# The first stretch of a decoder layer: a small table spread by the scalar engine, and the first batch's rotations on the vector engine

## The reference, cut to what matters

```python
def attn(x, Wq, Wkv_down, Wk_up, Wv_up):          # 16 heads of 32
    q = (x @ Wq)...                                # heads of 32: 8 plain numbers, 24 rotated ones
    c_kv = x @ Wkv_down                            # width 128
    k, v = (c_kv @ Wk_up)..., (c_kv @ Wv_up)...
    q_rope, k_rope = rope(q_rope), rope(k_rope)    # xe*cos - xo*sin, xo*cos + xe*sin
    scores = q @ k.T * scale, causal
    return softmax(scores) @ v
x = layernorm(x + attn(x))
x = layernorm(x + xattn(x, ctx))                   # top 54 of 512 keys
x = layernorm(x + ffn(x))                          # 8 experts, the first NL = 2 with low-rank additions
# gate[:NL] += x @ Ga @ Gb, up[:NL] += x @ Ua @ Ub, out[:NL] += mid @ Da @ Db
```

## Time and profile before

| | us |
|---|---|
| median of 3 runs | 1692.59 (1692.43 to 1700.83) |
| profiled execution | 1692.4 |
| its span | 1690.6 |
| start stretch, up to the first DVE instruction of the loop | 0 to 109.25 |

### The profile page before, as it was taken

How to read it: one execution, slowest core, us unless ns; L and a number is a source line. 1 busy time by engine, 2 the same in 40 slices (tenths; PEclk the granted TensorE clock), 3 DMA queues, 4 the chain that set the end, 5 groups by cost and what they waited for, 6 DMA issues and landing times.

```text
span 1690.6 us, 26867 instructions
## 1 busy us (share of the span) xinstructions
PE 1443.2 (85%) x9924; PEld 869.5 (51%) x9924; DVE 1273.0 (75%) x2115; ACT 903.6 (53%) x1431; POOL 846.8 (50%) x724
## 2 busy tenths in 40 slices
PE   4767787776668988848799999999999999999984
PEld 2345545444544444423356655666566655665553
DVE  4849899899867999975957767767766766766757
ACT  3327566565664544445455565556555565556542
POOL 6418385564352123687644654456454654466421
PEclk9969898989779999968999999999999999999997
DMA  9050010000211010110001000100101100100002
GB/s 282 26 200 2 28 51 2 28 26 27 100 51 50 26 70 32 51 63 13 25 26 38 26 26 29 35 26 26 37 26 31 33 26 26 38 26 26 13 1 100
DMA packets 63105, 74.62 MB, mean 44 GB/s; under 512 B 6912, under 2 KB 40320, under 8 KB 61952
## 3 DMA queue, kind: packets, MB, share of 16 engines
q1 hardware_dynamic: 62400, 68.68, 12.1%
q10 hardware_dynamic: 576, 4.19, 0.6%
HBM read 49.66 MB, written 10.49 MB: 36 GB/s over the span
## 4 chain that ended last, share of the span: by engine, by line
PE 60%; DVE 24%; issue 11%; ACT 3%; POOL 2%; DMA 1%; SPq 0%; DVEq 0%; POOLq 0%; ACTq 0%
PE banks L1103 48%; PE banks L870 6%; DVE nmf L1473 5%; DVE plo L1487 2%; PE banks L935 1%; DVE cat L1456 1%; PE banks L923 1%; DVE top L1599 1%; DVE wk L1595 1%; DVE att L1497 1%; DVE kcT L1463 1%; DMA w_fold<-w_top 1%; DVE attf L1606 1%; PE banks L1058 1%; DVE qcT L1483 1%
## 5 line engine op out<-in xcount | busy, mean ns | idle before, releaser
L1103 PE MATMUL banks<-xc,w 128*128 128x512 f16 x2688 | 591.2, 382 | 17.7 <-ACT banks L1144 15.0
L1103 PEld LDWEIGHTS banks<-xc,w 128*128 128x128 f16 x2688 | 264.2, 99 | 339.2 <-ACT banks L1144 20.2
L1103 PE MATMUL banks<-wd,mid 128*128 128x256 f16 x2688 | 298.1, 273 | 5.4 <-ACT banks L1144 3.1
L1103 PEld LDWEIGHTS banks<-wd,mid 128*128 128x128 f16 x2688 | 263.6, 98 | 40.9 <-ACT banks L1144 3.4
L847 POOL TENSOR_TENSOR mid<-m,mid 128x512 f16<-128x512 f32 x64 | 75.1, 1174 | 318.2 <-ACT mid L1144 318.2
L753 POOL TENSOR_TENSOR plo<-pf,phi 128x896 f16<-128x896 f32 x64 | 133.5, 2088 | 175.3 <-ACT phi L1144 175.2
L1144 ACT ACTIVATE banks<-banks 128x512 f32<-128x512 f32 x192 | 108.7, 579 | 193.0 <-PE banks L1103 193.0
L847 POOL TENSOR_TENSOR mid<-msum,mid 128x512 f16<-128x512 f32 x128 | 186.4, 1475 | 2.6 <-ACT mid L1144 2.6
L1421 DVE SCALAR_TENSOR_TENSOR w<-stage,w 128x512 f16<-128x512 f32 (+1 forms) x56 | 61.5, 1138 | 106.0 <-ACT w L1144 106.0
L1144 ACT ACTIVATE mid<-msum 128x512 f16<-128x512 f32 x128 | 81.2, 635 | 84.1 <-DVE msum L1780 28.1
L1473 DVE TENSOR_REDUCE nmf<-banks 128x1 f32<-128x512 f32 (+3 forms) x256 | 107.3, 480 | 14.9 <-PE banks L937 14.4
(11 more groups left out here) (252 smaller groups left out, 2910.8 us busy)
## 6 DMA issues: line engine op xcount, KB each, us to landing
stage<-w_fold SPq DMA_DIRECT2D x24, 256.0 KB, 3.0
stage<-in_Wg SPq DMA_DIRECT2D x24, 256.0 KB, 3.1
stage<-in_Wu SPq DMA_DIRECT2D x24, 256.0 KB, 3.1
stage<-in_Wd SPq DMA_DIRECT2D x24, 256.0 KB, 2.8
vcat<-vnext SPq DMA_DIRECT2D x8, 528.0 KB, 3.2
x_in<-in_x SPq DMA_DIRECT2D x4, 1024.0 KB, 6.3
x_res<-in_x SPq DMA_DIRECT2D x4, 1024.0 KB, 5.6
c_raw<-in_ctx SPq DMA_DIRECT2D x4, 1024.0 KB, 5.6
```

What stands on the lines that cost most here:

```text
L1103: mm = nc.tensor.matmul(out, l(x, i), r(y, i), start=start and i == 0 and j == 0, stop=stop and i == k - 1 and j == 2, skip_group_check=True)
```

## The change

Two edits.

1. POOL sets a table of only 4x16 (`own_small`), and ACT spreads it over the 512 columns of each head with one instruction of 4x8192. This stands in ACT's queue behind the four weights and ahead of `fold.0`. The sum of the semaphore `own_rows` is 3 instead of 2.
2. The eight rotations of the first batch are DVE's. POOL keeps those of the other three batches. `A_START_DVE` is written anew: eight `rope` steps are added, and `rlo`, `fold.0`, `v` and `cat0` stand in another order. The lists of PE and ACT for the stretch are the same.

```diff
 A_START_DVE = steps("""
-    half.0 half.1 c.0 rlo.0 rlo.1 fold.0 v.0 rlo.2 half.2 fold.1 v.1 rlo.3 half.3 fold.2 v.2 rlo.4 half.4 fold.3 rlo.5
-    half.5 fold.4 fold.5 cat0.0 cat0.1 cat0.2 cat0.3 cat0.4 rlo.6 cat0.5 rlo.7 cat0.6 cat0.7 maxn.0 maxn.1 maxn.2
-    maxn.3 v.3 mTn.0 maxn.4
+    half.0 half.1 rope.0 c.0 rope.1 rlo.0 fold.0 v.0 rope.2 rlo.1 half.2 rope.3 rlo.2 fold.1 v.1 rope.4 rlo.3 half.3 fold.2
+    v.2 rope.5 rlo.4 half.4 fold.3 rope.6 rlo.5 half.5 fold.4 rope.7 fold.5 cat0.0 rlo.6 cat0.1 cat0.2 cat0.3 rlo.7 cat0.4
+    cat0.5 cat0.6 cat0.7 maxn.0 maxn.1 maxn.2 maxn.3 v.3 mTn.0 maxn.4
 """)
...
-            own_row = kcT[K3:K3 + G, :, :].rearrange("p (g j) n -> p g j n", j=G)
+            own_row = own_small[K3:K3 + G, :].rearrange("p (g j) -> p g j", j=G)
             pool.wait_ge(consts, 14)
-            pool.memset(kcT[K3:K3 + G, :, :], 0.0).then_inc(own_rows, 1)
+            pool.memset(own_small[K3:K3 + G, :], 0.0).then_inc(own_rows, 1)
             pool.wait_ge(own_rows, 1)
             pool.affine_select(out=own_row, in_=own_row, compare_op=ALU.not_equal, fill=SNM, base=0,
-                               pattern=[[0, H // G], [-1, G], [0, S]], channel_multiplier=1).then_inc(own_rows, 1)
-
-            pool.wait_ge(own_rows, 2)
+                               pattern=[[0, H // G], [-1, G]], channel_multiplier=1).then_inc(own_rows, 1)
...
-            heads(next_part(A_POOL, A_NEXT), None, 0)
...
+            act.wait_ge(own_rows, 2)
+            scaled(kcT[K3:K3 + G, :, :], own_small[K3:K3 + G, :].unsqueeze(2).to_broadcast([G, H, S]), 1.0).then_inc(own_rows, 1)
...
+            def turn_row(i):
+
+                t = i // 2
+                if i == 0:
+                    dve.wait_ge(cossin_loaded, 16)
+                dve.wait_ge(a_drained["row"], a_upto(0, ("row", i)))
+                dve.wait_ge(roped, i * 4 + FREE)
+                pair = rows[:, i % 4, :, NOPE:HD].rearrange("p h (i two) -> p h i two", two=2)
+                for j, dst in ((0, turn_a), (1, turn_b)):
+                    cs = cossin[:, j, t].unsqueeze(1).to_broadcast([P, H, ROPE // 2, 2])
+                    tt_(dst[:, :, :, :], pair, cs, ALU.mult).then_inc(roped, 1)
+                dve.wait_ge(roped, i * 4 + (2 + FREE))
+                half = NOPE + ROPE // 2
+                tt_(rows[:, i % 4, :, NOPE:half], turn_a[:, :, :, 0], turn_a[:, :, :, 1], ALU.subtract).then_inc(roped, 1)
+                tt_(rows[:, i % 4, :, half:HD], turn_b[:, :, :, 1], turn_b[:, :, :, 0], ALU.add).then_inc(roped, 1)
```

More of the change, by code:

```diff
@@ L305, in decoder @@
         nm16 = sb(sa, "nm16", [P, TT, P], F16)
+        own_small = sb(sa, "own_small", [P, H], F16)
         qcT = sb(sa, "qcT", [P, H, S], F16)
@@ L948, in heads @@
                         if i == 0:
-                            pe.wait_ge(own_rows, 2)
+                            pe.wait_ge(own_rows, 3)
                         if i % G == 0:
@@ L1543, in _ @@
             for u in A_START_DVE:
-                if u[0] == "half":
+                if u[0] == "rope":
+                    turn_row(u[1])
+                elif u[0] == "half":
                     factor_lows(u[1])
```

## The result

| | median us | range | runs |
|---|---|---|---|
| kernel before | 1692.51 | 1691.14 to 1700.83 | 4 |
| changed kernel | 1706.15 | 1703.9 to 1710.03 | 4 |

The ratio of changed to before is 1.0075, with a 95% interval of 1.0043 to 1.0107. Run again beside 29 runs of the kernel before, 12 runs of the changed one gave 1.0048 (1.0029 to 1.0067), with medians of 1706.81 and 1698.44. By these two intervals the change makes the kernel slower by 0.3 to 1.1%. The forecast of 1697.6 was 8.6 us too low, and its range ended at 1703. In what follows one execution stood apart: of the six of the kernel "table late, POOL turns, PE fed late" one took 2990.26 us and the others 1679.33 to 1684.43; it is left out of the ratio, though not of the median, that its row gives.

The account below looks back on a forecast made before the run. The start stretch was taken to be bound by `v.3`, which lets the stores go, behind the end of `fold.5` and `cat0`. +4.0 at `fold.5` and +1.0 for two `rlo` gave +5.0 on 1692.6: 1697.6 us, range 1692 to 1703.

Parts of the forecast that it names:

- The table's removal from POOL: DVE's low half of `wq` no longer held by POOL's instruction: some 2.2 us, PE can start `row.0` 5.8 us sooner.
- The spread: ACT's 4x8192 instruction ahead of the factor halves takes 6.9 us; `row.0` drained at 26.5 instead of 28.34.
- PE's clock, c.0: After a gap of 3.7 us or more PE slows, c.0 takes 4.05 instead of 2.76: +1.3, bounds 0 and +2.3.
- The rival in which the clock stays up: c.0 stays at 2.76, total 1696.3; with all `maxn` at full clock too, 1694.2; chance 0.20.
- From c.0 to v.0 PE's chain is unchanged: PE's c, row.1, fold.0, row.2, v.0 stay as before and ahead of DVE; ACT's half of `v.0` ends at 41.6.
- a fall of the clock inside the folds: Sign of a wrong forecast: TensorE slows during the folds, where PE would then be late for DVE.
- The rotation: One rotation on DVE costs 1.61 us, bounds 1.48 and 3.0; six add 9.7 us.
- the rival of the dear rotation: Rotations on DVE cost more, deciding from 2.2 us each; at 3.0 the total is 1706; chance 0.08.
- DVE never idle behind v.0, 31.3 us: From `v.0` DVE works without a gap for 31.3 us; `fold.5` ends at 72.9 against 68.89, +4.0.
- The two rlo, +1.0: `rlo.6` and `rlo.7`, moved within `cat0`, no longer fill waits there: +1.0 us, bounds 0 and 1.2.
- maxn +0, with a bound of +1.4, and nothing for cat0: `maxn`, alternating PE and DVE without rotations, adds +0; -2.1 to +1.4 if the clock falls at another place.
- The clock further on: Later stages begin 5 us later; two or three half-speed stretches more or fewer give 1692.5 to 1702.7; chance 0.10.

Follow-up runs that it names:

- table late, POOL turns, PE fed late: Kernel before with ACT spreading the table just ahead of `v.3`, POOL keeping the rotations, 50 unread matmuls from around `fold.5` on: 0.9906 of before, again 0.9902.
- the rotations alone: Kernel before with only the rotations moved to DVE by its new list, POOL setting the table as before: 1.0034 of the kernel before.
- the table alone: Kernel before with only ACT's spread of the table ahead of the folds; POOL keeps the rotations, DVE its old list: 1.0004 of the kernel before.
- the late spread: Changed kernel with ACT's spread moved from ahead of the folds to just ahead of `v.3`: 1.0010 of the kernel before.
- the two `rlo` back: Changed kernel with `rlo.6` and `rlo.7` back behind `cat0.4` and `cat0.5`: 1705.14 us in a single execution.
- fed kernels: Changed kernel and kernel before, each with unread matmuls added where PE waits in the start stretch: 0.9976 and 0.9948 of the kernel before.
- profile 4: One further profiled execution of the kernel before, unaltered: 1699.19 us.
- the early 21 alone: Changed kernel with only 16 unread matmuls behind `row.0` and 5 behind `c.0`: 1.0056 of the kernel before.

## Why the prediction was wrong

- **The table's removal from POOL**: right. `wq`'s low half took 2.29 (2.2 predicted).
- **The spread**: 7.02 for a predicted 6.9 to 7.0, `row.0` drained at 26.75 (26.5). Right, and so was the loss of most of the gain to it.
- **PE's clock, c.0**: the mechanism was right, the size not. The term of +1.3 measured +2.3 to +2.5 in the four profiles (5.12, 5.05, 5.25 and 5.30 against 2.76). I had taken the 4.05 of `row.0`, where the clock came back on the way; the bound of +2.3 was the nearer one. The rival in which the clock stays up fell.
- **"From c.0 to v.0 PE's chain is unchanged"**: this step failed. `fold.0` and `row.2` took 4.50 and 4.36 instead of 2.76 each, +3.3 us, and so in three of the four profiles of the changed kernel. In the kernel before one of four shows the same (4.54 and 4.31). The wait ahead of `fold.0` is 1.50 in all eight, so the change did not lengthen it. Of the variants the rotations alone had this spell, and the table alone, the late spread and the two `rlo` back did not. Whether the change makes it more frequent, these few profiles can't tell. The prediction had named a fall of the clock inside the folds as a sign that it was wrong.
- **The rotation**: 1.59 us from start to start (1.61 predicted). Right, and with it the rival of the dear rotation fell.
- **DVE never idle behind v.0, 31.3 us**: 31.2. Right in all terms.
- **The two rlo, +1.0**: 0.9 at full clock, in the pair of fed kernels. At half speed, which the changed kernel has there, 0.3.
- **maxn +0, with a bound of +1.4, and nothing for cat0**: the second step that failed. Behind `fold.5` 3.4 us came on top of the forecast, all of it in stretches at half speed: 0.4 to the first copy, 1.6 in `cat0`, 0.7 to the first reduction and 0.7 in `maxn`. `cat0` at half speed is 2.2 us longer for the kernel before itself (9.86 in its profile 4, 7.66 in its first profile). I had given `maxn` a bound for the clock and `cat0` none, though PE waits in it for DVE after each turn. In all four profiles of the changed kernel both stretches lie at half speed; in the kernel before `cat0` does in two of four, and `maxn` wholly in two and in part in the other two (granted clock 0.60 and 0.67).
- **The base**: the forecast was set on a median of three runs, 1692.6, and on a profile of 1692.4. The medians of 29 and 31 runs are 1698.4 and 1698.7. Set on the 1698.4, the +5.0 would have given 1703.4, 3.4 under the measured 1706.8. In the first comparison three of the four runs of the kernel before took 1691 to 1693, as only 3 of those 31 did. Whether that was chance or the chip is open; it made the change look like 13.6 us, where the larger comparison makes it 8.4.
- **"The clock further on", 0.10**: this rival had half-speed spells of later stages come or go, two or three of 1.7 us. The spells that mattered lie in the start stretch. The rest behind it took 1581.5 to 1585.8 us in the four profiles of the changed kernel and 1579.1 to 1587.0 in those of the kernel before, which shows no difference. At `c.0`, `cat0` and `maxn` all four profiles of the changed kernel are at half speed.

What the 7.9 us consist of: 3 to 5 us of work that the edits add to the path (3.7 were predicted without the clock term), and the other 3 to 5 us of half speed that the kernel before also meets in some executions and the changed one in all four profiles. That the clock causes this second part is shown in the start stretch of the fed kernels, where it goes away without any change to ACT's or DVE's work: against the averages above, feeding takes 8.9 us from the stretch of the changed kernel and 3.7 from that of the kernel before, by one profile of each fed kernel. The medians do not show it as well. They fell by 0.72% in the one and 0.52% in the other, and the difference of 0.2% lies within the intervals. In both, about half of what feeding gained lies behind the stretch, where no matmul was added, and its cause stays open.

## What to carry to other kernels

Before a profile is used as the base of a sum, look at several executions of the same program: here the start stretch moved by 10 us with the clock alone, more than the change. When work goes from an engine off the path to one that TensorE waits for, price TensorE's work behind each longer wait at half speed, and the ping-pongs too; if a few unread matmuls can fill those waits in free banks, try them: 50 to 71 of them gave 0.5 to 0.7% in three kernels here, and the early 21 alone gave nothing that the median shows. A long one-off instruction belongs where its engine is idle, not ahead of the drains that PE waits for: the same 7 us put off c.0 by 3.7 us in one place (27.38 against 23.68), with the clock's price on top, and in ACT's idle time they held nothing up.

## What the runs showed of the hardware that was not expected

- TensorE's half-speed spells fell on different instructions in executions of one program. `fold.0` took 2.76 us in three profiles of the kernel before and 4.54 in the other, with the same wait of 1.50 us ahead of it.
- They followed gaps of 1.5 us too, not only of 4 (`fold.0` behind the 1.50 us wait for `cT`), when they came at all.
- The 16 added matmuls kept the clock at full speed over c.0 in both kernels that had them (2.76), against 4.45 to 5.30 in all six profiles with the gap left open.
